# A fused GNN and feed-forward kernel: layer 0's last tile by halves, own PSUM banks for the first gathered tiles, the last weight blocks in two pairs of banks, and the linear layer's first tile in another order

## The reference, cut to what matters

```python
x = x + linear(layernorm(x), W = scatter_add(edge_weight at (src, dst)), bias)   # layer 0, "gnn"
x = x + moe(layernorm(x))          # 8 experts, 2 per row, at most 314 rows per expert, hidden width 512
x = x + normalised_adjacency @ (layernorm(x) @ W1.T + b1)                         # layer 1, "gnn"
x = x + ffn(layernorm(x))          # 1024 -> 4096 -> 1024, ternary weights, rows quantised to 8 bits
```

## Time and profile before

| | before |
|---|---|
| median of 3 runs | 1021.59 us (1021.55 to 1022.98) |
| the profiled execution's own time | 1022.45 us |
| its span | 1020.7 us |
| PE busy in the span | 957.4 us (94%) |
| DVE, ACT, POOL busy | 758.3 (74%), 432.4 (42%), 211.0 (21%) |
| mean granted TensorE clock | 0.982 |

### The profile page before, as it was taken

How to read it: one execution, slowest core, us unless ns; L and a number is a source line. 1 busy time by engine, 2 the same in 40 slices (tenths; PEclk the granted TensorE clock), 3 DMA queues, 4 the chain that set the end, 5 groups by cost and what they waited for, 6 DMA issues and landing times.

```text
span 1020.7 us, 17357 instructions
## 1 busy us (share of the span) xinstructions
PE 957.4 (94%) x6685; PEld 528.4 (52%) x6685; DVE 758.3 (74%) x1095; ACT 432.4 (42%) x541; POOL 211.0 (21%) x203
## 2 busy tenths in 40 slices
PE   1799889999699999999979999999999999999998
PEld 0688745554466655555644434455544444444443
DVE  6999878786766666655778974587769768796874
ACT  5354435563255666655552211477634221222400
POOL 6300034221220001110033310010139990000000
PEclk9999899999699999999989999999999999999999
DMA  3900025554798888997645868499820555555672
GB/s 105 270 2 2 2 77 200 220 206 151 244 343 313 311 312 316 333 342 273 238 138 169 202 162 205 173 374 352 298 42 21 124 124 104 117 129 131 138 140 83
DMA packets 174850, 191.04 MB, mean 187 GB/s; under 512 B 135193, under 2 KB 135515, under 8 KB 170687
## 3 DMA queue, kind: packets, MB, share of 16 engines
q1 hardware_dynamic: 168383, 167.57, 52.5%
q0 software_dynamic: 6400, 22.55, 7.0%
HBM read 137.98 MB, written 36.38 MB: 171 GB/s over the span
## 4 chain that ended last, share of the span: by engine, by line
PE 87%; DVE 7%; issue 3%; DMA 1%; ACT 1%; DVEq 0%; POOL 0%; SPq 0%; ACTq 0%
PE ps L1167 20%; PE ps L1363 14%; PE ps L1436 9%; PE ps L1274 9%; PE ps L1345 8%; PE ps L1290 8%; PE ps L1387 3%; PE ps L1231 2%; PE ps L1023 1%; PE ps L1131 1%; DVE w1l L2211 1%; PE ps L1096 1%; PE ps L1041 1%; PE ps L1050 1%; DMA abs_e<-in_L_ffn_w 1%
## 5 line engine op out<-in xcount | busy, mean ns | idle before, releaser
L1363 PE MATMUL ps<-w1q,xqt 128*128 128x512 fp8e4 x640 | 139.3, 379 | 0.7 <-issue 0.7
L1753 ACT ACTIVATE hf<-ps,fs 128x512 f32<-128x512 f32 x80 | 54.9, 687 | 142.0 <-PE ps L1363 142.0
L1363 PEld LDWEIGHTS ps<-w1q,xqt 128*128 128x128 f16 x640 | 62.5, 98 | 76.0 <-issue 1.2
L870 POOL TENSOR_TENSOR rstd<-mv,consts 128x1 f32<-128x1 f32 (+1 forms) x40 | 29.0, 733 | 317.7 <-DVE mv L1880 230.1
L1167 PE MATMUL ps<-gwt_h,xt 128*128 128x512 f16 x320 | 84.6, 379 | 0.9 <-issue 0.9
L1167 PE MATMUL ps<-wt_h,xt 128*128 128x512 f16 x320 | 85.4, 379 | 0.0
L1274 PE MATMUL ps<-xdh,w1h 128*128 128x314 f16 x256 | 76.3, 298 | 3.0 <-DVE w1l L2211 2.7
L2461 DVE TENSOR_REDUCE hm<-hf 128x1 f32<-128x512 f32 x80 | 51.6, 680 | 35.3 <-ACT hf L1753 35.1
L1274 PE MATMUL ps<-xdh,w1l 128*128 128x314 f16 x256 | 75.8, 296 | 0.0
L1274 PE MATMUL ps<-xdl,w1h 128*128 128x314 f16 x256 | 75.6, 295 | 0.0
L1345 PE MATMUL ps<-hs_h,at_h 128*128 128x512 f16 x200 | 59.5, 379 | 0.8 <-DVE hs_l L2429 0.8
(11 more groups left out here) (342 smaller groups left out, 2120.0 us busy)
## 6 DMA issues: line engine op xcount, KB each, us to landing
wstage<-in_L_ffn_w SPq DMA_DIRECT2D x32, 1024.0 KB, 7.0
abs_in<-in_L_ffn_w SPq DMA_DIRECT2D x18, 1024.0 KB, 6.6
abs_e<-in_L_ffn_w SPq DMA_DIRECT2D x14, 1024.0 KB, 5.2
fnat_b<-in_L_ffn_w SPq DMA_DIRECT2D x28, 512.0 KB, 8.0
fnat_a<-in_L_ffn_w SPq DMA_DIRECT2D x27, 512.0 KB, 6.3
hq_d<-hq SPq DMA_DIRECT2D x18, 512.0 KB, 4.8
eo_d<-eo SPq DMA_DIRECT2D x16, 512.0 KB, 3.0
xs_d<-xs_all SPq DMA_DIRECT2D x10, 512.0 KB, 2.9
```

Of the source, the lines that this page charges most:

```text
L870: g.tensor_tensor(rstd[:, one], mv[:, one, 1], consts[:, 1:2], ALU.pow).then_inc(s_rstd, 1)
L1363: last = mm(ps[:, n % 4, :], xqt[:, u, k, :], w1q[:, k // 2, n * 512:(n + 1) * 512, k % 2], start=(k == 0), stop=(k == KD - 1))
L1753: cp(hf[:, i % 2, n * 512:(n + 1) * 512], ps[:, n % 4, :], ACT.Gelu, scale=fs[:, i % 2, 3:4]).then_inc(s_ge, 1)
```

## The change

Seven edits, in the order of the program. The diff below is cut to its core.

1. Layer 0, tile 9: PE makes columns 0 to 511 first, then the logits, then columns 512 to 1023. The DVE (`last_gnn0`) adds and takes the statistics of the first half, does `gate_terms(1)`, then the second half.
2. Routing: one operation (`rt - 1`) goes, by comparing with a shifted iota, and the subtraction on `scan_o` stands ahead of `y_low(9)`.
3. Expert 0's three gathered tiles get their own pairs of banks (4 and 5, 1 and 2, 6 and 7). `split_low(0, 1)` moves behind the three copies.
4. Every expert: the first product waits only for the high weights. In each hidden block the 16 matmuls with `w1h` come first, then the 8 with `w1l`, and the wait for `w1l` stands there in block 0.
5. SP sends the first half of an expert's third result tile when that half is ready, not when both are.
6. Last expert: weight blocks 5 and 7 go to banks 0 and 1, and the three `ranked` products come behind all blocks.
7. Linear layer: `kept_busy(8)` becomes `kept_busy(4)`, `norm` of tile 0 stands ahead of `mixed(1, 0)`, and `low` and `copy_low` of tile 0 ahead of `mixed(1, 1)` and tile 1's statistics. Tile 1's transposes come at step 5 of tile 0's product (before, 3). POOL issues each pair of gathers one place earlier against `rstd`.

```diff
@@ SP, expert results
-                    sp.wait_ge(s_g2r, 3 + 6 * e + 2 * s + 2)
+                    sp.wait_ge(s_g2r, 3 + 6 * e + 2 * s + (2 if s < 2 else 1))
...
+                        sp.wait_ge(s_g2r, 3 + 6 * e + 2 * s + 2)
                         sp.dma_start(rows[:, 512:D], eo[64:64 + 48, u, 512:D]).then_inc(s_eoh[u], 16)
@@ POOL, gathers of expert results
-                if n % 2 == 1 and n >= 3:
-                    rstd_tile(2 * NT + n // 2 - 1, n // 2 - 1)
+                if n % 2 == 1 and n >= 5:
+                    rstd_tile(2 * NT + n // 2 - 2, n // 2 - 2)
+            rstd_tile(3 * NT - 2, NT - 2)
             rstd_tile(3 * NT - 1, NT - 1)
@@ PE, product
+                if n == R_LIN1 - 1:
+                    for h in range(2):
+                        for k in range(KD):
+                            for a, (lhs, rhs) in enumerate(((xth, rh), (xth, rl), (xtl, rh))):
+                                last = mm(ps[:, 2 * u + h, :], lhs[:, u, k, :], rhs[:, k, h * 512:(h + 1) * 512],
+                                          start=(k == 0 and a == 0), stop=(k == KD - 1 and a == 2))
+                        if h == 0:
+                            logits_of(n, u)
+                    last.then_inc(s_mm, 1)
+                    return
...
+                    if k == (5 if n == R_LIN1 else 3) and n not in (R_LIN1 - 1, R_LIN1 + NT - 1) and not by_transfer(n + 1):
                         transposes(n + 1, 1 - u)
@@ PE, expert
-                pe.wait_ge(s_wl, 4 * e + 2)
+                pe.wait_ge(s_wh, 4 * e + 2)
                 for hb in range(KH):
...
+                    if hb == 0:
+                        pe.wait_ge(s_wl, 4 * e + 2)
...
@@ PE, last expert
-                        if i < KD - 1:
-                            ranked(i - 4, (6, 7, 3)[i - 4])
+                    for h, bank in enumerate((6, 7, 3)):
+                        ranked(h, bank)
...
-            kept_busy(8)
+            kept_busy(4)
@@ DVE, layer 0's last tile
+            def last_gnn0(i, u):
+                cols = [slice(h * 512, (h + 1) * 512) for h in range(2)]
+                dve.wait_ge(s_lg, NT)
+                do(v.scalar_tensor_tensor(out=x[:, i, cols[0]], in0=ps[:, 2 * u, :], scalar=1.0 / (SX * SW),
+                                          in1=x[:, i, cols[0]], op0=ALU.mult, op1=ALU.add))
...
+                v.bn_stats(stats[:, 0, :], x[:, i, cols[0]]).then_inc(s_bn, 1)
+                dve.wait_ge(s_const, 14)
+                gate_terms(1)
+                dve.wait_ge(s_mm, 1 + R_GNN0 + i + 1)
...
@@ DVE, start of the linear layer
             mixed_statistics(0)
+            norm(R_LIN1, 0, 0)
             mixed(1, 0)
-            norm(R_LIN1, 0, 0)
+            low(R_LIN1, 0)
+            copy_low(R_LIN1, 0)
             mixed(1, 1)
-            low(R_LIN1, 0)
             mixed_statistics(1)
-            copy_low(R_LIN1, 0)
```

More of the change, by code:

```diff
@@ L1232, in gathered, with first_rows @@
                     last.then_inc(done, 1)
+            def first_rows(s):
+                m = SM[s]
+                pe.wait_ge(s_g[s], 16)
+                for part, done in enumerate((s_gth, s_gtl)):
+                    for k in range(KD):
+                        c = part * D + k * P
+                        last = tr(bank16(FIRST_BANKS[s] + part)[:, k * P:k * P + m], gx[0:m, s, c:c + P], id16[0:m, 0:m])
+                    last.then_inc(done, 1)
             def w1_t(i):
@@ L1272, in expert @@
                     for k in range(KD):
[L1273 to L1275 removed]
+                        for a, rhs in enumerate((xdh, xdl)):
+                            mm(ps[:, 6 + hb % 2, 0:CAP], w1h[:, k, hb * P:(hb + 1) * P], rhs[:, k, :],
+                               start=(k == 0 and a == 0), stop=False)
+                    if hb == 0:
+                        pe.wait_ge(s_wl, 4 * e + 2)
+                    for k in range(KD):
+                        last = mm(ps[:, 6 + hb % 2, 0:CAP], w1l[:, k, hb * P:(hb + 1) * P], xdh[:, k, :],
+                                  start=False, stop=(k == KD - 1))
                     last.then_inc(s_g1, 1)
@@ L2323, in _ @@
             split_low(0, 0)
[L2324 removed]
+            for s in range(3):
+                gathered(0, s, FIRST_BANKS[s] + 1)
             split_low(0, 1)
[L2326 to L2327 removed]
             for q in range(2, 4):
```

58 lines of the change are left out of this document (33 added, 25 removed).

## The result

| | before | changed |
|---|---|---|
| median of 20 runs | 1022.07 us (1020.78 to 1028.11) | 1026.12 us (1021.71 to 1030.73) |
| the profiled execution | 1022.45 us, span 1020.7 | 1028.18 us, span 1026.5 |
| mean granted clock | 0.982 | 0.978 |

The changed kernel is slower by 0.41% (ratio 1.0041, 95% interval 1.0030 to 1.0051). The forecast was 1019.5 us with a range to 1021.0. Its runs lie 9 us apart from the fastest to the slowest (7.3 us before, 3.2 us without one run at 1028.11), and the profiled execution is 2 us above its median.

A forecast was written before the change was run, and what follows sets the result against it. PE, busy for 94% of the span, was taken as the bound, so only its waits could give time. Terms 1.7 + 0.9 + 0 - 0.5 = 2.1 us less took the median from 1021.59 to 1019.5 us, range 1017.3 to 1021.0.

The forecast's parts named there:

- End of layer 0 and expert 0: Layer 0's last tile, routing and expert 0's gathers and banks: 1.7 us less together, bounds 0.9 and 2.4.
- The seven changes of expert: Waits for w1l between experts go, but ACT's abs_e pass holds block 2: 0.9 us less, bounds 0.3 and 2.8.
- The last expert's 0.6 us: Change to the last expert, which has no abs_e pass: an earlier first block wins 0.6 us.
- SP's earlier store of half a result tile hides beside PE's work: In the experts: the earlier store of half a result tile is hidden beside PE's work.
- Start of the linear layer: Earlier gathers and rstd against a longer DVE order up to tile 2: 0 us, bounds -1.9 and +0.8.
- the slack at tile 4: Linear layer: 0.4 us between tile 4's transposed rows landing and its product takes up the DVE's 0.3 us lateness.
- The clock: Low clock at tile 0's transposes may delay the DVE 1.1 us; half taken, 0.5 us lost, bounds 0 and -1.1.
- The slower one: Linear layer: earlier gathers collide with writes and transposing reads of tiles 3 to 8; 1026.6 us, chance 0.08.
- The waits of the experts count in full: Experts: abs_e lands earlier or ACT reaches it sooner, and the clock stays high; 1017.0 us, chance 0.15.
- the fourth rival: End of layer 0 gives nothing, as PE's one-column matmuls or a store hold the gathers; 1020.7 us, chance 0.05.

The follow-up runs named there:

- before_edit4: Kernel before with edit 4 alone: matmuls with the high weights first, the wait for the low ones behind them; 1023.30 us, ratio 1.0017.
- pass_and_old_start: Changed kernel with ACT's second abs_e pass behind its reading of block 0 and edit 7 undone (old linear-layer start); 1015.63 us, ratio 0.9941.
- before_pass_behind: Kernel before with only ACT's second pass over abs_e moved behind its reading of block 0; 1019.94 us, ratio 0.9977.
- w1l_wait_first: Changed kernel with edit 4 undone: an expert's first product waits for both weight halves, matmuls in the old order; 1027.93 us, ratio 1.0046.
- edits_1_to_3: Kernel before with edits 1 to 3 alone; 1023.80 us, ratio 1.0016.
- after_abs_e_sooner: Changed kernel with the second transfer of abs_e sent ahead of the store of the second result tile; 1023.57 us, ratio 1.0010.
- store_late: Changed kernel with edit 5 undone: SP sends the third result tile when both halves are ready; 1028.96 us, ratio 1.0058.
- pass_behind_block0: Changed kernel, all edits kept, with ACT's second pass over abs_e behind its reading of the next expert's block 0; 1018.54 us, ratio 0.9962.
- new_start_old_pool: Changed kernel with ACT's pass behind block 0, DVE's and PE's new linear-layer start, POOL's gathers behind rstd as before; 1018.94 us, ratio 0.9973.

## Why the prediction was wrong

- **End of layer 0 and expert 0, 1.7 us.** The trace gives 1.5, and its parts are off by little. The logits came 0.43 us sooner against the product, not 0.75. The row shows what I left out: 0.46 us from the end of POOL's `rstd` at 255.16 + 0.55 to the DVE's start.

```profile
255.16 0.55 POOL L873 TENSOR_TENSOR rstd<-mv,consts 128x1 f32<-128x1 f32 x1 [10.08 <-DVE mv L2175]
```
```profile
256.17 0.17 DVE L2148 TENSOR_TENSOR logits<-lg,rstd 128x16 f32<-128x16 f32 x1 [0.67 <-POOL rstd L873]
```

  In expert 0 nothing was given back: expert 0 to expert 1 took 28.85 us. But I treated the moved split as free except for 0.4 us. It is only so with edit 4. And in the time of edits 1 to 3 alone the 1.5 us don't show.
- **The seven changes of expert, 0.9 us less.** This is the step that failed. "There PE was already held, and an earlier first block wins nothing, since the transfer is issued behind the second result tile and doesn't move" has the right place and the right queue. It is half of the result: nothing won. The other half I did not price, because I took one landing of before for a constant. From 1 to 7 the experts took 5.7 us more, not 0.9 less. In the changed kernel the transfer took 0.04 to 1.9 us longer than in the same expert before (3.1 in before_edit4), nearly all of it went into PE's wait (1.91 and 2.04 us at experts 1 and 6, where `abs_e` took 7.0 and 7.1), and one wait of 2 us brought a stretch of low clock. My bounds (0.3 and 2.8 us, both gains) excluded a loss without a reason. The last expert's 0.6 us was also more than it waited (0.5). Whether "SP's earlier store of half a result tile hides beside PE's work" holds stays open: without it the waits at block 2 were up to 0.4 us shorter in four of six experts, and the time was not.
- **Start of the linear layer, 0.** It cost 2.1 us, and edit 7 alone 3.2 us by the ratio (3.4 in its trace). The pieces: `rstd` in 0.57 us as forecast; the second addition 1.1 us earlier, not 1.5; from tile 0's `norm` to tile 2's 4.1 us more, not 2.8 (the terms as written add up to 2.9). The wait for PE's low transposes was in the sum with 0.8 us and took 2.00, since both sets of transposes ran at the low clock. That is the term that was mis-sized. The DVE's stream was 2.0 us late, not 0.3, and PE waited at tiles 2 and 3, not 4. Only the slack at tile 4 had been looked up.
- **The clock, 0.5.** The low stretch lies over tile 0's transposes (533.67 to 540.50), so the whole 1.1 us was due. It is the 1.2 us more of the wait above, and not to be counted twice. That is what the page of the Trainium skill that the prediction cites (TensorE: Matmul & The Clock Gate, "What's actually happening") would have given, and this trace agrees with it: 0.50 for 6.8 us, from 0.7 us behind an idle stretch of 2.02 us on. With eight fillers and idle stretches of 1.85 and 1.65 us there (pass_and_old_start) no low stretch came. The costs of the clock inside the experts were not in the sum at all.
- **The rivals.** The slower one named the wrong place: the collision of gathers with tile 3's and 4's rows is worth 0.1 to 0.2 us. "The waits of the experts count in full" needed the pass behind block 0: then 3.4 us come (174.19 to 170.75), as before_pass_behind and the experts of 28.46 us show. In the fourth rival, 1020.7 us leaves out the 0.5 us of the clock: with it, 1021.2.

## What to carry to other kernels

When a wait is removed, look up the next one on the same path, and price it with the spread of what releases it, not with one row. If it ends with a transfer, the landing can slip, and an engine that arrives earlier pays the whole slip. The cure is often a place in a list: an operation that nobody waits for (here the pass over `abs_e`) must not stand ahead of one that frees a bank. Moving it won 2.3 us in the kernel before and 7.6 us in the changed one. And an edit that is free only because of another (the moved split) must be tested with and without it.

## What was not expected of the hardware

- A transfer of 1 MB that took 5.2 to 5.7 us at experts 1 to 6 before took up to 8.4 in other kernels, often with a single late completion of sixteen. A load of instructions stood near the start of most of the late ones, but not of all.
- A stall of PE of 2.0 to 3.3 us at or in an expert went with a granted clock of 0.50 for 3.4 or 6.8 us in five profiles (changed, before_edit4, w1l_wait_first, edits_1_to_3, after_abs_e_sooner), and with none at other stalls of the same length (expert 1 of store_late, 2.2 us). So the same stall costs 2 us in one execution and 4 in another. The spread of the runs doesn't follow from it: it is 9 us for the changed kernel and 4 for pass_behind_block0, but also 9 for pass_and_old_start and new_start_old_pool, which have no such stall in the experts. What spreads them was not looked for.
